# Masked cross attention: head outputs and softmax sums moved by DMA, divided on folded sums

## What is computed

```python
# per batch b: target = x[b], source = context[b], both (256 channels, 512 positions)
q = (Wq @ target + bq) * target_mask      # and k, v of the source; 16 heads of 16 channels
score = q_h.T @ k_h / sqrt(16) with the masks' -1e6 terms
out_h = softmax(score) @ v_h              # 16 channels x 512 positions for each head
x = layernorm(x + out * target_mask)
```

## Time and profile before

| | |
|---|---|
| median of 3 runs | 3759.37 us (3742.02 to 3769.1) |
| the profiled execution | 3762.4 us |
| its span | 3760.6 us |
| TensorE busy | 3136.6 us, 83% |
| VectorE busy | 1814.3 us, 48% |
| ScalarE busy | 1270.2 us, 34% |
| GpSimd busy | 443.6 us, 12% |
| mean granted clock of TensorE | 0.934 |

### The profile page before, as it was taken

One profiled execution on the slowest core, in us unless ns is written; L12 is line 12 of the kernel. 1 busy time (PEld: TensorE's weight loads), 2 busy tenths in 40 slices (PEclk: granted clock), 3 DMA queues, 4 the chain that ended last, 5 costly groups with the idle time before them and its releaser, 6 DMA issues. The chain is left out here.

```text
span 3760.6 us, 48775 instructions
## 1 busy us (share of the span) xinstructions
PE 3136.6 (83%) x16434; PEld 2042.4 (54%) x16467; DVE 1814.3 (48%) x3379; ACT 1270.2 (34%) x3220; POOL 443.6 (12%) x469
## 2 busy tenths in 40 slices
PE   6999657887887489999978888599999997799894
PEld 4666412222222167777755554588888886444441
DVE  5666646666666321112216666466676664211113
ACT  2333224445545201111104443455565553111110
POOL 1000100000000200000010000233333332300002
PEclk9999868889989799999989999799999998999997
DMA  1000144444443400000010000311121113500323
GB/s 68 12 22 23 40 76 72 70 77 74 76 68 51 123 19 12 12 12 18 12 42 21 19 21 16 98 40 45 62 79 52 45 34 141 203 0 34 123 89 109
DMA packets 128286, 207.68 MB, mean 55 GB/s; under 512 B 9720, under 2 KB 60376, under 8 KB 128128
## 3 DMA queue, kind: packets, MB, share of 16 engines
q1 hardware_dynamic: 111424, 166.86, 17.4%
q0 software_dynamic: 7664, 27.40, 2.1%
q10 hardware_dynamic: 9040, 11.33, 1.0%
HBM read 146.87 MB, written 58.29 MB: 55 GB/s over the span
## 5 line engine op out<-in xcount | busy, mean ns | idle before, releaser
L1148 DVE TENSOR_REDUCE x_minus_max<-banks 128x2 f32<-128x1024 f32 x256 | 308.9, 1221 | 180.4 <-PE banks L1256 177.4
L1093 ACT ACTIVATE x_probs<-banks 128x512 f32<-128x512 f32 x512 | 290.8, 596 | 284.5 <-PE banks L1274 211.8
L1274 PE MATMUL banks<-x_stacked_q,x_stacked_k 105*128 105x512 bf16 x512 | 210.0, 421 | 76.0 <-ACT x_probs L1093 55.0
L481 ACT ACTIVATE a_probs<-banks,a_minus_max 128x128 f32<-128x128 f32 (+1 forms) x512 | 208.6, 425 | 145.4 <-DVE a_minus_max L564 143.8
L1256 PE MATMUL banks<-x_stacked_k,x_stacked_q 102*128 102x512 bf16 x512 | 175.1, 428 | 90.1 <-DMA x_stacked_k<-x_mask_parts_dram 65.4
L1274 PEld LDWEIGHTS banks<-x_stacked_q,x_stacked_k 105*128 105x128 bf16 x512 | 50.8, 100 | 296.1 <-ACT x_probs L1093 189.6
L2755 DVE TENSOR_TENSOR m_h<-banks,m_silu 128x512 f32<-128x512 f32 x39 | 27.0, 692 | 317.8 <-PE banks L2871 165.5
L2085 ACT ACTIVATE x_probs<-banks,x_minus_max,x_rroot 128x256 f32<-128x256 f32 x256 | 142.9, 566 | 91.6 <-DVE x_minus_max L2196 91.6
L1593 DVE TENSOR_TENSOR f_hT<-banks,f_silu 128x256 f32<-128x256 f32 (+1 forms) x88 | 37.3, 424 | 280.2 <-ACT f_silu L1519 280.2
L564 DVE TENSOR_REDUCE a_minus_max<-banks 128x2 f32<-128x512 f32 (+1 forms) x192 | 131.8, 687 | 82.2 <-remote 55.4
L2021 POOL TENSOR_TENSOR x_probs<-x_probs,x_inverse 128x512 f32<-128x512 f32 x128 | 133.1, 1040 | 274.4 <-DVE x_inverse L2230 274.4
(11 more groups left out here) (377 smaller groups left out, 7767.9 us busy)
## 6 DMA issues: line engine op xcount, KB each, us to landing
x_x<-x_after SPq DMA_DIRECT2D x24, 512.0 KB, 4.4
x_parts_dram<-x_parts SPq DMA_DIRECT2D x16, 768.0 KB, 8.8
x_stacked_q<-x_parts_dram SPq DMA_DIRECT2D x48, 256.0 KB
x_stacked_k<-x_parts_dram SPq DMA_DIRECT2D x48, 256.0 KB
x_after<-a_z SPq DMA_DIRECT2D x16, 512.0 KB, 2.8
x_after<-x_z SPq DMA_DIRECT2D x16, 512.0 KB, 3.1
x_context<-in_ctxT SPq DMA_DIRECT2D x16, 512.0 KB, 5.4
m_w<-in_m_g SPq DMA_DIRECT2D x8, 1024.0 KB, 5.7
```

Source lines behind the costliest of these rows:

```text
L481: ins = act.activation(probs[:, n % 3, i * width:(i + 1) * width], psum[uses.bank(use)][:, i * width:(i + 1) * width], ACT.Exp, bias=minus ...
L1093: act.activation(probs[:, n % 8, :], psum[at.bank(f"exp{n}")], ACT.Exp, scale=SCALE)\
L1148: dve.tensor_reduce(minus_max[:, c % 2, h % 4, 2 * (n % 2):2 * (n % 2) + 2], at.pair(use), AX.X, ALU.max, negate=True)\
L1274: ins = pe.matmul(psum[at.bank(use)], stacked[1][u][:, h, s * P:(s + 1) * P], stacked[0][u][:, h, :], start=True, stop=True)
```

## The change

`finish`, its one-hot table and their five operations on VectorE are gone. ScalarE's copy of each group is followed by eight DMAs of SyncE (`move_heads`): four bring the rows of sums to DRAM, four bring 16 rows of a head each into `heads`. When both groups of a half are there, one DMA folds the sums to 32 partitions x 128 (`fold_sums`), VectorE takes the reciprocal of that (slot 43 for the first half, slot 9 of the next batch for the second), and SyncE writes it to DRAM and spreads it by eight DMAs over 16 partitions each (`spread_inverse`). GpSimd multiplies, masks and adds x (`combine`), with x and the mask loaded a second time into `z` and `out_mask` (`load_rows`). The statistics follow on VectorE at slot 58, and at slot 28 of the next batch; normalise at its slot 34.

The projections are cut: each half of q and k at slots 1, 5, 9, 13, those of v at 31 and 37, all in bank 7. GpSimd takes both subtractions of the split. SyncE's order is written out per batch, the semaphores of the stage are cleared behind it, and the first two batches stand ahead of the loop. `load_inputs(1, 1)` goes out ahead of the first stack.

```diff
-            if q in (36, SLOTS + 3):
-                add(("finish", 0 if q == 36 else 1))
+PIECES_AT = (1, 5, 9, 13)
+VALUES_AT = (31, 37)
+        for n, start in enumerate(PIECES_AT):
+            for kind, at in (("project'", 0), ("whole'", 2), ("round'", 3), ("again'", 6)):
+                if q == start + at:
+                    add((kind, n))
...
+        for step, at in ((("inverse''", 1), 9), (("stats''", 1), 28), (("normalise''", 0), 34), (("inverse", 0), 43), (("stats", 0), 58)):
+            if q == at:
+                add(step)
...
@@ sync
+            def load_rows(b, u):
+                sp.dma_start(z[:, u], x_src[b].rearrange("(j p) d -> p j d", p=P)).then_inc(z_loaded[u], 16)
+                sp.dma_start(out_mask[:, u, :], mask[b].unsqueeze(0).broadcast_to([P, POS])).then_inc(z_loaded[u], 16)
...
+            def move_heads(b, u, c):
+                n, half = c // 2, c % 2
+                sp.wait_ge(heads_copied, b * 4 + (c + 1))
+                for i in range(4):
+                    sp.dma_start(sums_dram[u, n, 4 * half + i:4 * half + i + 1, :], heads_out[32 * i + CH:32 * i + CH + 1, half, :])\
+                        .then_inc(heads_moved[half], 16)
+                for i in range(4):
+                    sp.dma_start(heads[64 * half + CH * i:64 * half + CH * (i + 1), n, :], heads_out[32 * i:32 * i + CH, half, :])\
+                        .then_inc(heads_moved[half], 16)
+            def fold_sums(b, u, n):
+                for half in range(2):
+                    sp.wait_ge(heads_moved[half], (b * 2 + (n + 1)) * MOVES)
+                sp.dma_start(sums[:, n, :], sums_dram[u, n].rearrange("h (k f) -> (h k) f", f=P)).then_inc(sums_loaded, 16)
+            def spread_inverse(b, u, n):
+                sp.wait_ge(inverted, b * 2 + (n + 1))
+                sp.dma_start(inverse_dram[u, n].rearrange("h (k f) -> (h k) f", f=P), inverse[:, n, :]).then_inc(inverse_written, 16)
+                sp.wait_ge(inverse_written, (b * 2 + (n + 1)) * 16)
+                for h in range(H // 2):
+                    sp.dma_start(inverse_rows[CH * h:CH * (h + 1), n, :], inverse_dram[u, n, h].unsqueeze(0).broadcast_to([CH, POS]))\
+                        .then_inc(inverse_loaded, 16)
...
-                for w in range(2):
-                    stack(w, b + 1, 1 - u)
-                store(b, u)
-                load(b + 2, u)
+                if prev:
+                    move_heads(b - 1, 1 - u, 3)
+                    fold_sums(b - 1, 1 - u, 1)
+                if own:
+                    if not (isinstance(b, int) and b < 2):
+                        sp.wait_ge(stored[u], at.in_turn * 16)
+                    load_rows(b, u)
+                if prev:
+                    spread_inverse(b - 1, 1 - u, 1)
+                if own:
+                    move_heads(b, u, 0)
+                if following:
+                    for w in range(2):
+                        stack(w, b + 1, 1 - u)
+                if own:
+                    move_heads(b, u, 1)
+                    fold_sums(b, u, 0)
+                if prev:
+                    store(b - 1, 1 - u)
+                if own and not (isinstance(b, int) and b + 2 >= B):
+                    sp.wait_ge(v_ready, b * 2 + 2)
+                    load_inputs(b + 2, u)
+                if own:
+                    spread_inverse(b, u, 0)
+                    move_heads(b, u, 2)
@@ gpsimd
+            def take_rest(b, n):
+                pool.wait_ge(first_part, b * 4 + (n + 1))
+                pool.tensor_tensor(rest[:, w, m, :], whole[:, w, m, :], parts[:, w, 0, m, :], ALU.subtract).then_inc(rest_ready, 1)
...
+            def combine(b, u, n, loads):
...
+                pool.wait_ge(inverse_loaded, (b * 2 + (n + 1)) * 16 * (H // 2))
+                pool.tensor_tensor(heads[:, n, :], heads[:, n, :], inverse_rows[:, n, :], ALU.mult).then_inc(combine_steps, 1)
+                pool.tensor_tensor(heads[:, n, :], heads[:, n, :], out_mask[:, u, :], ALU.mult).then_inc(combine_steps, 1)
+                pool.tensor_tensor(z[:, u, n, :], heads[:, n, :], z[:, u, n, :], ALU.add).then_inc(combine_steps, 1)
+            def run(steps, at, b, u):
+                if following:
+                    for n in range(4):
+                        take_rest(b + 1, n)
+                        take_third(b + 1, n)
+                if prev:
+                    combine(b - 1, 1 - u, 1, at.loads(-1))
+                    pool.wait_ge(moved, b * NORM_STEPS)
+                    pool.tensor_tensor(rstd[:, :], vareps[:, :], core.minus_half[:, 0:TT], ALU.pow).then_inc(rstd_ready, 1)
+                if own:
+                    combine(b, u, 0, at.loads(0))
@@ scalar, the copy of a group
+                        if not (isinstance(b, int) and b == 0 and c < 2):
+                            act.wait_ge(heads_moved[c % 2], (b * 2 + c // 2) * MOVES)
                         act.copy(heads_out[:, c % 2, :], psum[6]).then_inc(free[6], 1)
+                        act.sem_inc(heads_copied, 1)
@@ vector
+                    if kind in ("inverse", "inverse''"):
+                        dve.wait_ge(sums_loaded, (owner * 2 + (n + 1)) * 16)
+                        dve.reciprocal(inverse[:, n, :], sums[:, n, :]).then_inc(inverted, 1)
+                    if kind in ("stats", "stats''"):
+                        dve.wait_ge(combine_steps, (owner * 2 + (n + 1)) * (COMBINE_STEPS // 2))
+                        dve.bn_stats(stats[:, n, :], z[:, of, n, :]).then_inc(moved, 1)
@@ decoder_layers
+        core.release_semaphores()
```

More of the change, by code:

```diff
@@ L884, in listed @@
                 out.append((f"{tag}context{n // 4}", 6))
[L885 to L892 removed]
+        return out
+    lead, start, middle, last, end = (xattn_schedule(*there) for there in (
+        (False, False, True), (False, True, True), (True, True, True), (True, True, False), (True, False, False)))
     ring = [0]
[L894 to L895 removed]
+    before = BankUses(core.uses, listed("a", lead, ring), 1)
+    opening = BankUses(before.after, listed("0", middle, ring) + listed("1", middle, ring), 1)
+    looped = BankUses(opening.after, listed("0", middle, ring) + listed("1", middle, ring), TURNS - 2)
     ending = BankUses(looped.after, listed("0", middle, ring) + listed("1", last, ring), 1)
@@ L982, in pair, with loads @@
                 return core.banks[:, self.bank(use):self.bank(use) + 2, :]
+            def loads(self, ahead):
+                if isinstance(self.b, int):
+                    return (self.b + ahead) // 2 + 1
+                return self.in_turn + (1 + (self.u + ahead) // 2)
         def every_sequence(engine, run):
-            run(first_steps, At(before, "a", 0, -1, 1), -1, 1)
-            with engine.Fori(0, TURNS - 1) as turn:
+            run(lead, At(before, "a", 0, -1, 1, None), -1, 1)
+            run(start, At(opening, "0", 0, 0, 0, 0), 0, 0)
+            run(middle, At(opening, "1", 0, 1, 1, 0), 1, 1)
+            with engine.Fori(0, TURNS - 2) as turn:
                 for u in range(2):
[L990 to L993, removed]
+                    b = turn * 2 + (u + 2)
+                    run(middle, At(looped, str(u), turn, b, u, turn + 1), b, u)
+            run(middle, At(ending, "0", 0, B - 2, 0, TURNS - 1), B - 2, 0)
+            run(last, At(ending, "1", 0, B - 1, 1, TURNS - 1), B - 1, 1)
+            run(end, At(None, "", 0, B, 0, TURNS), B, 0)
         block = ctx.enter_context(nc.Block())
@@ L1034, in _ @@
                     sp.dma_start(mask_dram[w, :, j, :], mask_parts[:, w, pair[w], :]).then_inc(mask_written, 16)
[L1035 to L1040, removed]
-                for w in range(2):
-                    stack(w, b + 1, 1 - u)
-                store(b, u)
-                load(b + 2, u)
[L1047 to L1053, removed]
+            load_inputs(1, 1)
+            def run(steps, at, b, u):
+                prev, own, following = ("stats''", 1) in steps, ("exp", 0) in steps, ("project'", 0) in steps
+                if not prev and not own:
+                    sp.wait_ge(mask_written, 16 * 2 * len(PAIRS))
+                if prev:
[23 more added lines that the diff above has]
+                    move_heads(b, u, 2)
+            every_sequence(sp, run)
             for u in range(2):
-                sp.wait_ge(norm.stored[u], 16 * TURNS + 1)
+                sp.wait_ge(stored[u], 16 * TURNS)
         @block.gpsimd
```

298 lines of the change are left out of this document (133 added, 165 removed).

## The result

The changed kernel takes 3787.4 us (3783.4 to 3798.5, 5 runs) against 3759.2 of the kernel before: a ratio of 1.0084, with 1.0052 to 1.0117 as its 95% interval. Run again in the last group of experiments it took 3790.3, ratio 1.0080 (1.0057 to 1.0104). So 28 us more, where 23 (3783) were forecast.

A forecast was written before the change was run, and what follows sets the result against it. Each batch was taken as bound by a DMA chain, then the slots from 42 to the next 17. Terms 8.4 + 6.4 - 4.0 - 6.3 + 12.7 + 5 + 1 = +23 on 3759.4 gave 3783 us, range 3732 to 3845.

The forecast's parts named there:

- The chain and its lateness: Per batch, write of q's parts to next batch's first score: 40.4 us of DMAs, starting 6.4 us later after slot 17.
- The first finish gives nothing, the second 7 us: Per batch: removal at slot 36 only lengthens the wait for k's stacks; removal behind slot 42 saves 7.0 us.
- the exponentials: TensorE's wait for ScalarE, 7.0 us per batch: 1 us comes back (bounds 0 and 2).
- first DMA to first score: Start: loads of batch 1 now stand ahead of q's first parts, +5 us (bounds 2 and 9).
- first score to first write: Ahead of the first write of q's parts: the later start of the chain, +6.4 us.
- six times score to next write: Six batch periods at +1.4 us each: later chain start and new waits against savings, +8.4 us.
- last score to last store: End of the stage: savings of 4.0 and 6.3 us against a tail longer by 12.7, together +2.4.
- The new waits: Per batch at slot 43 (inverse), slot 58 (stats) and for rows of maxima: 1 us each, 3.0 together (0 to 9).
- The rows of maxima at slot 48: Rows of maxima of slot 43 travel in the same DMA burst: 1 us per batch (bounds 0 and 1.5).
- the rival of late sums: TensorE's lead does not cover slots 43 and 58: 9 us per batch instead of 3, 3825 us; chance 0.30.
- The tail: From the last group's copy to the store: 24.1 us instead of 11.4, +12.7 (bounds 9 and 16).
- The landings: DMA time from issue to landing, taken as 2.05 us after the last of 12 small writes in the earlier trace.

The follow-up runs named there:

- e1: Changed kernel with SyncE's move_heads of group 0 placed behind both stacks of a batch; 3716.7 us, ratio 0.9892.
- e2: Changed kernel where SyncE still waits for group 0's copy ahead of the stacks but issues the eight moves behind them; 3758.1 us, ratio 0.9997.
- e3: Kernel before, without the products, reciprocal, scaling and masking of each batch's first finish; 3755.6 us, ratio 1.0001.
- e4: Kernel before, without the products, reciprocal, scaling and masking of each batch's second finish; 3696.1 us, ratio 0.9843.
- e8: Changed kernel with VectorE's whole' in the slot of project' itself instead of two slots later; 3765.3 us, ratio 1.0015.
- e7: As e6, with VectorE's inverse at slot 47 instead of 43 and stats at 61 instead of 58; 3716.8 us, ratio 0.9881.
- e6: As e1, with whole' one slot after project' and batch 1's loads behind the first stacks; 3709.6 us, ratio 0.9876.
- e10: As e9, with the eight spreads of the second half's inverses issued while the write of q's parts is landing; 3694.0 us, ratio 0.9824.
- e9: As e6, with whole' in the slot of project' itself; 3714.5 us, ratio 0.9883.

## Why the forecast was right, point by point

**The chain and its lateness.** Right in the mechanism. The write leaves 6.1 us behind slot 17's product (766.91 against 760.83) where 5.5 were forecast, the chain is 0.5 us longer than it was, and e1 and e2 show that this, and not the work on the engines, is where the gain went. The waiting fell elsewhere than announced: the first score waits 11.5 us for k's stacks, not 12 to 16, and the rows of maxima take 6.4 us more than before. The period of 98.4 us lies just above the 93 to 98 that were named.

**The first finish gives nothing, the second 7 us.** Right for the first (e3); the second gives 8.0 (e4).

**The sum by stretches**, from the two profiles:

| stretch | forecast | measured |
|---|---|---|
| first DMA to first score | +5 | 67.1 to 70.3, +3.2 |
| first score to first write | +6.4 | 38.5 to 49.4, +10.9 |
| seven chains, write to score | 0 | 280.6 to 284.2, +3.6 |
| six times score to next write | +8.4 | 324.8 to 347.3, +22.5 |
| last score to last store | +2.4 | 106.9 to 102.0, -4.9 |
| rest of the kernel | +1 | +0.8 |

The sum is +36 against +23; between the medians it is +28. The term that was mis-sized is the fourth: 3.8 us per batch where 1.4 were forecast. The prediction let the pieces of the projections cost nothing and named no wait for bank 7, in which all four of them and the transposes of the maxima now stand in one row: 3.1 us per batch, and e8 got 25 us back by taking that away, 1.3 us per batch of it as pieces that no longer run at the lower clock (46.4 us of pieces in six batches where the changed kernel has 54.1). The second row holds the same wait once. Against these stand gains that were taken too small: 8.0 instead of 7.0 us for the second finish, and 2.0 instead of 1.0 for the exponentials (30.0 us in six batches, 42.1 before). That +28 (+36 between the profiles) came so near to +23 is in part luck: missed costs and missed gains offset each other. The new waits were put at 3.0 in all; they came out otherwise than split. At slot 43 VectorE waits 0.4 us for the folded sums in this batch (at most 0.8) and at slot 58 not at all:

```profile
810.88 0.94 DVE L1285 RECIPROCAL x_inverse<-x_sums 32x128 f32<-32x128 f32 x1 [0.38 <-DMA x_sums<-x_sums_dram]
...
829.49 0.68 DVE L1289 BATCH_NORM_STATS2 x_stats<-x_z 128x6 f32<-128x512 f32 x1
```

GpSimd had the sums combined in time, though its subtractions and products take 1.16 and 1.27 us where I had taken 1.04 from another stage:

```profile
L1137 POOL TENSOR_TENSOR x_rest<-x_whole,x_parts 128x512 f32<-128x512 f32 x26 | 30.1, 1156 | 117.3 <-ACT x_parts L1209 116.3
L1154 POOL TENSOR_TENSOR x_heads<-x_heads,x_out_mask 128x512 f32<-128x512 f32 x16 | 20.4, 1274 | 1.6 <-POOL x_heads L1151 0.7
```

The rows of maxima at slot 48 cost 1.7 to 3.2 us instead of 1 (bounds 0 and 1.5). So the rival of late sums did not come: TensorE's table has no wait for a pair's maxima, through which VectorE's would have had to pass; and moving the sums later (e7, on top of e6) changed nothing.

The range's upper end was added up wrongly: with its own bounds a batch is +9.4 and the sum about +90 (3850), not +96 (3855). Nothing hangs on it.

**The tail.** From the copy of the last group to the store are 21.8 us, 24.1 were forecast and 11.4 it was the earlier trace rows:

```profile
1284.31 0.59 ACT L1227 COPY x_heads_out<-banks 128x512 f32<-128x512 f32 x1 [1.27 <-PE banks L1352]
```

```profile
1306.14 0.39 SPq L1037 DMA_DIRECT2D x_after<-x_z  x1
```

The landings were taken too long. The forecast had 2.05 us from the row at 480.36, but that write waited for VectorE too, whose third part ends at 480.28:

```profile
479.06 1.22 DVE L1181 TENSOR_TENSOR x_parts<-x_rest,x_parts 128x1024 bf16<-128x1024 f32 x1 [1.11 <-ACT x_parts L1111]
```

So it was an upper bound. In the tail the fold is read 1.7 us after its issue (2.5 forecast), the inverses are spread 1.4 us after their write (2.5), and moves and spreads take 5.0 and 5.1 us (5.8 each); GpSimd's three steps take 4.0 us (3.1).

The rest of the last stretch gave 15.3 us back instead of 10.3. e4 alone, without the second finishes, is 15.3 us shorter from the last score to the last store, e3 2.9; how the two add up in the changed kernel no run shows.

**The clock.** The granted clock of the six batches, 0.86 against 0.89, was in no step. The mean does not decide: e8 has 0.85 and is 25 us faster. What the clock costs shows in the length of like products. Scores, exponentials' products and context products take 416, 419 and 675 ns on average, 421, 420 and 688 before. Only the pieces became slower, and by the comparison with e8 that is 1.3 us per batch, some 9 us in seven batches (an estimate from the two profiles).

**What stays open.** Why the last piece of k is slow in four of the six batches and not in the other two; and half a microsecond per batch between two executions of the same kernel (98.4 and 97.9).

## What to carry to other kernels

Ask of each saving which wait ends last behind it. The same products were worth 61 us on one side of a DMA wait and nothing on the other. And when steps move to the engine that issues the DMAs, look at what stands behind them in its order: put the issue that starts the longest chain ahead of those that only have to be done sometime, and use the time in which it waits for a landing. A gain counts only while its wait is the bound: the same edit to `whole'` was worth 25 us in the changed kernel and nothing once the chain started early.

## What was not expected of the hardware

ScalarE sends the maxima in three DMAs of 4 KB, on a queue of its own. Beside a burst of SyncE's they are slow. In the changed kernel those of slot 27 leave at 771.93, 1.1 us after the first of the six stacks of q (770.82), and TensorE goes on at 785.20, 13.3 us later.

```profile
771.93 1.81 ACTq L1204 DMA_DIRECT2D x_stacked_q<-x_max_rows  x3
```

In the kernel before they left 13.4 us after the first of such a burst (846.49), and TensorE went on after 5.0 us:

```profile
859.93 1.81 ACTq L1103 DMA_DIRECT2D x_stacked_q<-x_max_rows  x3
```

```profile
864.93 0.39 PE L1274 MATMUL banks<-x_stacked_q,x_stacked_k 105*128 105x512 bf16 x1 [1.30 <-DMA x_stacked_q<-x_max_rows]
```

So here a second queue is no way past a burst that has just been issued; no run moves the rows alone, and how the two queues share the DMA engines is not shown. In the changed kernel it presumably cost little, since TensorE waits for k's stacks behind it in any case (9.95 us in that batch); this is argued and not run. In e1 and e10, with that wait shorter, the rows of maxima are up to 4.2 and 3.6 us of waiting at a time, and in e9 they take most of what was gained at bank 7.
